# A two-layer graph network on one core: twelve dense chunks and three sums placed earlier in the first pass, and the nodes' own weighted terms added by VectorE instead of TensorE

## The reference

```python
h = max(layernorm(x), 0)
# layer 0: messages weighted by w_e, summed over the edges that end in a node
msg = h[dst] @ W_i + h[src] @ W_j + edge_attr @ W_e
x = x + segment_sum(w_e * msg, dst) + h @ W_self
h = max(layernorm(x), 0)
# layer 1, twice: mean over the neighbours, a product, a bias
h = relu(mean(h[src]) @ W1_l.T + b1 + h @ W1_r.T)
h = mean(h[src]) @ W2_l.T + b2 + h @ W2_r.T
x = x + log_softmax(h)
```

## Time and profile before

| | us |
|---|---|
| median of three runs | 1644.01 |
| profiled execution | 1642.16 |
| its span | 1640.3 |
| PE busy | 1422.1 |
| DVE busy | 971.8 |
| ACT busy | 605.0 |
| POOL busy | 716.3 |

### The profile page before, as it was taken

One profiled execution on the slowest core, in us unless ns is written; L12 is line 12 of the kernel. 1 busy time (PEld: TensorE's weight loads), 2 busy tenths in 40 slices (PEclk: granted clock), 3 DMA queues, 4 the chain that ended last, 5 costly groups with the idle time before them and its releaser, 6 DMA issues.

```text
span 1640.3 us, 26156 instructions
## 1 busy us (share of the span) xinstructions
PE 1422.1 (87%) x8546; PEld 1019.2 (62%) x8547; DVE 971.8 (59%) x4416; ACT 605.0 (37%) x1493; POOL 716.3 (44%) x769
## 2 busy tenths in 40 slices
PE   2588788788797988979879998999999979999996
PEld 0366666666575665756656668566666656666664
DVE  7798999997798987979798866200101130010204
ACT  5355565564645466455663346200000010020203
POOL 8777777776677776667676745000000000000000
PEclk9688899899998999989999999999999989999999
DMA  8477777888989888999889983687777748777773
GB/s 265 141 232 258 252 262 258 277 283 282 305 266 313 278 287 276 287 317 280 283 290 316 326 277 152 247 317 285 274 286 273 288 160 313 268 306 271 295 281 135
DMA packets 178854, 441.28 MB, mean 269 GB/s; under 512 B 24619, under 2 KB 104924, under 8 KB 175388
## 3 DMA queue, kind: packets, MB, share of 16 engines
q1 hardware_dynamic: 155996, 391.75, 66.4%
q0 software_dynamic: 22432, 46.97, 10.9%
q10 hardware_dynamic: 288, 0.85, 0.1%
HBM read 318.94 MB, written 120.55 MB: 268 GB/s over the span
## 4 chain that ended last, share of the span: by engine, by line
PE 64%; DVE 11%; DMA 10%; ACT 9%; issue 2%; POOL 2%; SPq 1%; DVEq 0%; ACTq 0%; POOLq 0%
PE psAE L1132 32%; PE psAE L1042 14%; DMA home<-h_table 8%; PE psAE L1074 6%; ACT home L789 4%; DVE home L1432 4%; PE psW L936 4%; DVE home L1436 3%; PE psW L1051 2%; DVE home L1490 2%; PE psW L1061 2%; ACT home L821 1%; PE psNS L1051 1%; PE psAE L1040 1%; ACT home L832 1%
## 5 line engine op out<-in xcount | busy, mean ns | idle before, releaser
L631 POOL DMA_INDIRECT home<-h_table,src_i x676 | 656.5, 971 | 266.4 <-issue 200.2
L1132 PE MATMUL psAE<-home 128*128 128x350 f16 x3528 | 538.2, 313 | 5.7 <-DVE home L1534 3.7
L1132 PEld LDWEIGHTS psAE<-home 128*128 128x128 f16 x3528 | 337.9, 96 | 200.9 <-issue 3.7
L1042 PE MATMUL psAE<-home 128*128 128x256 f32 x1352 | 322.9, 398 | 26.4 <-DVE home L1466 10.0
L1042 PEld LDWEIGHTS psAE<-home 128*128 128x128 f32 x1352 | 268.4, 201 | 78.8 <-issue 33.4
L1490 DVE TENSOR_SCALAR home<-iota_h,dst_rel,home 128x128 f32<-128x128 f16 x832 | 222.1, 363 | 17.2 <-PE psAE L1042 14.7
L1432 DVE TENSOR_SCALAR home<-iota_h,tile 128x245 f16<-128x245 f16 x1004 | 209.7, 303 | 27.7 <-PE psW L1061 18.8
L789 ACT ACTIVATE home<-psW 128x490 f16<-128x490 f32 x406 | 206.1, 577 | 51.7 <-PE psW L1051 38.7
L1436 DVE TENSOR_SCALAR home<-iota_h,tile 128x128 f16<-128x128 f16 x1004 | 179.3, 280 | 0.0
L1051 PE MATMUL psW<-home 128*128 128x245 f16 x812 | 126.0, 287 | 37.0 <-DVE home L1436 34.5
L1588 DVE SCALAR_TENSOR_TENSOR home<-psAE,home 128x350 f32<-128x350 f32 x18 | 9.4, 523 | 243.3 <-PE psAE L1132 238.5
(11 more groups left out here) (213 smaller groups left out, 1197.9 us busy)
## 6 DMA issues: line engine op xcount, KB each, us to landing
home<-counts SPq DMA_DIRECT2D x36, 4287.5 KB, 13.4
counts<-home SPq DMA_DIRECT2D x126, 612.5 KB, 4.8
home<-edges SPq DMA_DIRECT2D x64, 845.0 KB
weighted<-home SPq DMA_DIRECT2D x24, 1225.0 KB, 6.5
home<-weighted SPq DMA_DIRECT2D x36, 800.0 KB
home<-h_table,src_i POOLq DMA_INDIRECT x676
home<-h_table SPq DMA_DIRECT2D x36, 256.0 KB
home<-inv_row SPq DMA_DIRECT2D x36, 175.0 KB, 13.1
```

The costliest lines, as they stand in the source:

```text
L631: pool.indirect_dma_start(out=rows[to][:, j, :], out_offset=None, in_=from_table[:, :], in_offset=bass.IndirectOffsetOnAxis(ap=src_i[b][:, ...
L1042: done = nc.tensor.matmul(psA[:, 0:2 * P].rearrange("p (n f) -> p n f", n=2), onehot[:, j, :], both_of(s, b, j), start=(j == 0), stop=(j = ...
L1132: last = nc.tensor.matmul((psA, psE)[r][:, 0:SNODES].rearrange("p (c d) -> p c d", c=SUPER), halves[:, a, n, :], tiles[:, :, a, :], start= ...
```

## The change

Two things change. First, the tables of the first pass: the dense turns come earlier, and the three groups' pieces have other spans. Dense turns are now 3, 6, 9, 12, 16, 20, 25, 30, 35, 39, 44 and 49: the stretches from one to the next have 3 turns three times, 4 turns three times and 5 turns five times. Turns 50 to 63 are fourteen sourced ones. The first two groups' 26 pieces lie in turns 15 to 48, the last group's 13 in turns 50 to 62: two in turns 52 and 57, none in 51, one in each of the others. Second, the own weighted term leaves TensorE: GpSimd scales all 49 blocks, in order, and VectorE adds them to `x_sb`, one instruction of 7 blocks (896 columns) a step, and waits for its end before it adds the products. ScalarE's 14 scalings and TensorE's 49 identity matmuls are gone. (A single launch, the same inputs and outputs.)

```diff
-DENSE_AFTER = (2, 5, 9, 12, 16, 19, 23, 27, 30, 34, 38, 41)
-PIECE_SPANS = ((14, 29), (29, 43), (43, 51))
+DENSE_AFTER = (2, 4, 6, 8, 11, 14, 18, 22, 26, 29, 33, 37)
+PIECE_SPANS = ((11, 25), (25, 40), (40, 51))
...
                 pool.wait_ge(weight_kept, 1)
-                pool.wait_ge(own_back[1], 16)
-                for t in range(OWN_FIRST, BLOCKS):
-                    pool.tensor_scalar(accN[:, t * FEATS:(t + 1) * FEATS], accN[:, t * FEATS:(t + 1) * FEATS], node_weight[:, t:t + 1], None,
-                                       ALU.mult).then_inc(own_scaled, 1)
+                for n, (lo, hi) in enumerate(OWN_PARTS):
+                    pool.wait_ge(own_back[n], 16)
+                    for t in range(lo * UNROLL, hi * UNROLL):
+                        pool.tensor_scalar(accN[:, t * FEATS:(t + 1) * FEATS], accN[:, t * FEATS:(t + 1) * FEATS], node_weight[:, t:t + 1], None,
+                                           ALU.mult).then_inc(own_scaled, 1)
...
-                act.wait_ge(weight_kept, 1)
-                act.wait_ge(own_back[0], 16)
-                for t in range(OWN_FIRST):
-                    nc.scalar.activation(accN[:, t * FEATS:(t + 1) * FEATS], accN[:, t * FEATS:(t + 1) * FEATS], ACT.Copy,
-                                         scale=node_weight[:, t:t + 1]).then_inc(weight_kept, 1)
...
-                    if own:
-                        t = s * UNROLL + at + n
-                        if t < OWN_FIRST:
-                            pe.wait_ge(weight_kept, t + 2)
-                        else:
-                            pe.wait_ge(own_scaled, t - OWN_FIRST + 1)
-                        last = nc.tensor.matmul(bank[:, n * FEATS:(n + 1) * FEATS], ident[:, :], accN[:, columns], start=False, stop=True)
...
-            def first_rows():
+            def first_rows(scaled_own=False):
 
                 for s in range(STEPS + 2):
                     if s < STEPS:
+                        if scaled_own:
+                            own_columns = slice(s * UNROLL * FEATS, (s + 1) * UNROLL * FEATS)
+                            x_rows = x_sb[:, s * UNROLL:(s + 1) * UNROLL, :].rearrange("p t f -> p (t f)")
+                            dve.wait_ge(own_scaled, (s + 1) * UNROLL)
+                            nc.vector.tensor_tensor(x_rows, x_rows, accN[:, own_columns], ALU.add).then_inc(own_added, 1)
+                            dve.wait_ge(own_added, BLOCKS + s + 1)
```

More of the change, by code:

```diff
@@ L100 @@
 OWN_PARTS = ((0, 2), (2, 7))
-OWN_FIRST = OWN_PARTS[0][1] * UNROLL
 assert BLOCKS + OWN_ADDED < CHUNKS
@@ L929, in _, with products @@
                      1: ((hT, W1_R), (accA, W1_L)), 2: ((hT, W2_R), (accA, W2_L))}
-            def products(s, q, terms, bank, own=False):
+            def products(s, q, terms, bank):
                 at, width = PARTS[q]
@@ L936, in products @@
                         last = nc.tensor.matmul(bank[:, n * FEATS:(n + 1) * FEATS], frm[:, columns], w_sb[:, w, :],
-                                                start=(k == 0), stop=(k == len(terms) - 1 and not own))
-                    if own:
-                        t = s * UNROLL + at + n
-                        if t < OWN_FIRST:
-                            pe.wait_ge(weight_kept, t + 2)
-                        else:
-                            pe.wait_ge(own_scaled, t - OWN_FIRST + 1)
-                        last = nc.tensor.matmul(bank[:, n * FEATS:(n + 1) * FEATS], ident[:, :], accN[:, columns], start=False, stop=True)
+                                                start=(k == 0), stop=(k == len(terms) - 1))
                 return last
@@ L1106, in _, with mix_first @@
             fast = pe.value_load(fast_row[0:1, 0:1], min_val=0, max_val=1)
-            def mix_first(terms, own=False):
+            def mix_first(terms):
                 for s in range(STEPS + 2):
@@ L1115, in mix_first @@
                                 pe.wait_ge(mix_read[0], (s - 2) * UNROLL + at + width)
-                            products(s, q, terms, psB[s % 2 * 2 + q], own).then_inc(mixed[0], width)
+                            products(s, q, terms, psB[s % 2 * 2 + q]).then_inc(mixed[0], width)
                     if 2 <= s < LATE + 2:
@@ L1140, in _ @@
                 pe.wait_ge(added[0], ADDED)
-                mix_first(TERMS[0], True)
+                mix_first(TERMS[0])
                 for p in PASSES:
@@ L1623, in _ @@
                     nc.vector.memset(mark[:, p - 1:p], 0.0).then_inc(super_read[p], 2)
-                first_rows()
+                first_rows(True)
                 dve.wait_ge(deg_in, 16)
```

## The result

The changed kernel took 1662.46 us (median of four, 1659.42 to 1670.03), the kernel before, beside it, 1643.09 us (1641.2 to 1646.68): ratio 1.015, 95% interval 1.0116 to 1.0183, slower by 19 us between the medians and by 24.6 (19 to 30) by the ratio, which takes in further executions of the changed kernel, all between 1660 and 1675 us. A later comparison of the same two kernels gave 1.0109 (1.0081 to 1.0136), +18 us by the ratio and +16 between the medians. The forecast was +10.3 us: the sign was right, the size about half of what was measured.

A forecast was written before the change was run, and what follows sets the result against it. The first pass was taken as bound by compute, with late gathers bounding its end after the change; 12.8 us lost less 2.5 us gained gave +10.3 us, 1652.5 us on the profiled execution, 1654.3 us on the median, range 1637 to 1664.

The forecast's parts named there:

- What bounds the kernel: First pass: the compute side sets the pace, 12.1 us a sourced turn; GpSimd's 16.4 us sets have 5.6 us in reserve.
- The pieces: First pass: 26 pieces cost 36.7 us, mostly TensorE's load waits; cost kept for the new tables, bounds zero to 52.8 us.
- The last fourteen turns: First pass's end: gathers set the pace, turn 63 starting 193.2 us after turn 50, 12.8 us later than before.
- The compute side: Turns 50 to 63: compute work alone needs 180.7 us, hidden by the gathers' 193.2 us.
- Turn 50's start: First pass: turn 54's old start less four sourced turns of 12.1 us, 794.8 us; up to 3 us more allowed.
- The own term: Mixing stage: moving the own weighted term to GpSimd and VectorE gains about 2.5 us, bounds -4.5 to +1.
- TensorE's side of the round: Mixing stage: without identity matmuls the two-step chain of waits falls from 13.24 to 11.7 us, 5.8 a step.
- The shared port: Mixing stage: VectorE and GpSimd blocking each other would cost some 3 us; set aside because the trace does not show it.
- The sum: Whole kernel: 12.8 us lost in the first pass, 2.5 us gained in the mixing stage, +10.3 us.
- (1): Rival, turns 15 to 48: piece waits shrink with the earlier start, kernel faster; half the cost gone gives 1636; 14%.
- (2): Rival: GpSimd's lag is mostly made good by faster gathers, mixing and pieces, no change, 1644 to 1648 us; 20%.
- (3): Rival, ahead of turn 50: dense turns two sourced ones apart cost 5 us and more extra, 1660 to 1672 us; 10%.

The follow-up runs named there:

- the tables alone: Kernel before with only the new tables of dense turns and pieces, own weighted term unchanged: 1668.97 against 1645.39 us, 1.0136; on another chip 2013.01 against 2012.19 us.
- the end of them alone: Kernel before with tables changed only behind sourced chunk 23 (dense turns closer, last pieces over 11 turns): 1662.71 us, 1.011; on another chip 2012.64 us, 0.9989.
- the gathers thinned: Changed kernel, last twelve sets fetching 12 of 13 tiles: 1646.23 against 1637.08 us for the kernel before, 1.0054; on other chips 0.9913, 0.9917, 0.9924.
- the own term alone: Kernel before with only the own weighted term moved to GpSimd and VectorE, tables unchanged: 1644.14 us, 1.0; on another chip 2010.98 us, 0.9988.
- The spare matmuls: Kernel before with the own weighted term moved and six unused matmuls per mixing step: 1634.08 against 1635.75 us, 0.9992; on other chips 0.9985, 0.9988.
- early front: Kernel before with the first eight dense turns as in the changed kernel, last four and last pieces unchanged, own weighted term unchanged: 0.9991 and 1.0013.
- half the dose: Kernel before with the last dense turn after sourced chunk 39 instead of 41, twelve sourced turns at the end, own weighted term unchanged: 0.9977.

## Why the prediction was right or wrong

**What bounds the kernel** was read rightly: a set of gathers at 16.4 us against a sourced turn at 12.1 us, with dense turns as the balance and three sets as the limit of what can be saved up.

**The pieces were misread.** The 52.8 us of waits in the earlier trace rows add the idle time of the matmuls and that of the weight loads, which wait side by side. The matmuls alone, 330 to 843 us:

```profile
  DMA home<-h_table: 24.4, 12
```

and 3.6 us in 5 from there to turn 63. So the loads explain some two thirds of the 36.7 us that the first 26 pieces cost, and little of the 16.6 us of the last 13. Also, by the tables, the second group's last piece lies in turn 53 in the kernel before and in turn 50 in the changed one: 25 pieces lie ahead of turn 50 and 14 behind, where 26 and 13 were counted. Neither decides the forecast.

**The last fourteen turns: right.** Forecast 193.2 us from turn 50 to turn 63; measured 194.0, 192.5, 193.8 and 193.3 in four profiles on short chips (the changed kernel twice, the tables alone, the end of them alone). The kernel before took 131.95 us for the ten last turns; with four more at 12.1 us, 13.0 us of the loss lie here. Of the terms, the ten sets took 165.0 to 166.2 us (forecast 164.2 + 1.3 - 0.3 = 165.2). The second set began 24.6 to 24.7 us behind turn 50 in three profiles and 26.6 in one, instead of 26.1, and turn 63 came 2.1 to 3.3 us behind the last gather, instead of 1.9: two small errors that cancel, which was luck. In each of the four, every set from that one on began right behind the one before, ten sets long, where the kernel before has six. The compute side, put at 180.7 us, was too high: with the gathers thinned the stretch took 183.0 us, of which TensorE waited 12.2 us for gathers, and turns with one piece take as little as 11.8 us (53, 54 and 56 in the first profile of the changed kernel), where 13.4 was counted. It didn't matter, as the gathers hide it.

**Turn 50's start: the step that failed,** a mis-sized term. The prediction put it at 843.24 - 4 x 12.1 = 794.8 us. Five profiles on short chips have (the changed kernel twice, the tables alone, the end of them alone, the thinned one) 797.9, 801.7, 806.1, 802.0 and 799.5, mean 801.5: 6.7 us more. The subtraction keeps all that lay ahead of turn 54, its last dense turn too, which took 11.4 us. In the same five profiles that turn, now 49, took (start to start) 20.3, 17.7, 20.2, 16.1 and 18.5 us: 18.6 on average, 7.2 us more. This difference is clear of the spread: with the tables of before turn 53 took 11.4, 11.3 and 11.7 us in the three profiles on short chips. The stretches ahead of turn 49 cost on average what they should: 31, 38, 41 and 34 us over the sum without pieces in the four profiles with the changed tables, and 41 with the end of them alone, where 36.7 was carried over. But that average rests on values that lie far apart; with the tables of before the same figure is 37, 47 and 30 us, and turn 54 begins at 843.2, 853.8 and 836.8. So turn 49 accounts for the surplus of the mean, not for that of one profile.

I had seen that 11.4 was low, and allowed 3 us in the bounds, by an average over all turns. The rows of before would have given the number. Its dense turns with a piece (21, 25, 30, 35, 39, 44, 49, 53) take 15.7 us on average, and the three of them that follow a turn without a piece (21, 30, 44) take 19.1, 18.4 and 18.2, 18.6 on average. Turn 49 of the changed tables has a piece and follows a turn without one. What TensorE waits for in turn 49 of the second profile, in the middle of the turn:

```profile
792.04 0.40 PE L982 MATMUL psW<-home,ones 128*1 128x100 f32 x2 [3.47 <-ACT home L789]
...
797.26 2.95 PE L1062 MATMUL psAE<-home 128*128 128x400 f32 x8 [1.22 <-DMA home<-h_table]
```

ScalarE had itself waited 4.67 us for a store to `counts` there. In all eight profiles on short chips the 25 dense turns with a piece behind a turn without one take 17.7 to 20.5 us, and the 39 behind a turn that has one 11.2 to 17.6. So the tables' pattern of pieces goes with most of the loss here; no run changed it alone, so it isn't shown to be the cause. And it can't be all of it: in the end of the tables alone, turn 49 follows a turn with a piece, and took 16.1 us, 4.7 more than 11.4.

**The own term: the gain was put too high.** -2.5 us forecast. In the two profiles of the changed kernel the part behind turn 63 is 3.3 and 1.0 us shorter than in the kernel before, in the own term alone 0.3 us; over all profiles of each kind the gain is 0.9 us, and the time of the own term alone is 0.0% (4 us either way). The step that failed is the 5.8 us a step for TensorE's side of the round. The round of 11.7 us does occur, in the first profile of the changed kernel:

```profile
1017.29 5.21 PE L931 MATMUL psW<-w_sb,home 128*128 128x128 f32 x28
...
1030.09 0.95 PE L920 MATMUL psNS<-ident,home 128*128 128x128 f32 x7 [3.20 <-ACT home L860]
1030.88 3.29 PE L931 MATMUL psW<-w_sb,home 128*128 128x128 f32 x28
...
1041.76 0.95 PE L920 MATMUL psNS<-ident,home 128*128 128x128 f32 x7 [1.88 <-ACT home L860]
```

From 1030.09 to 1041.76 us it takes 11.67 us. But the sum took the matmuls off and kept the clock. With fewer of them the granted clock of this half fell to 0.91 here, 0.85 in the second profile and 0.87 in the own term alone, and in one step of each the 28 product matmuls took 4.4 to 5.2 us instead of 3.29 (above, at 1017.29). A step at that time or later then takes 7.2 to 7.8 us, longer than the 6.7 of before. Where the low clock reached the next stage, as in the own term alone, its 98 matmuls took 1.5 us more too. The spare matmuls brought the clock to 0.94 and above and left no step over 6.4 us behind the first: the stage's end (second group of line 1132, 1120 and 1122) came 68.2 to 69.8 us behind turn 63, where the kernel before has 72.4. The kernel's own spread limits this: two runs with the own term as before (early front once, half the dose), have 70.6 and 70.3. So the clock's part is shown in the rows, and not in the time.

**The shared port.** The Trainium skill (SBUF — State Buffer, "Who interferes with whom") calls the ports that the two engines share an exclusive lock. The prediction set this aside because VectorE's line 1534 took 1.06 us with GpSimd busy and without. That looked at one side only. GpSimd's rows in the kernel before show the other, one beside the instruction at 1002.80 and one beside that at 1009.47:

```profile
1003.10 1.23 POOL L684 TENSOR_SCALAR home<-home,node_weight 128x128 f32<-128x128 f32 x1
...
1009.52 1.48 POOL L684 TENSOR_SCALAR home<-home,node_weight 128x128 f32<-128x128 f32 x1
```

Its others take 0.59 to 0.60 us. So the two contend, as that section says, and for GpSimd a lock fits the rows, here and in the changed kernel (2.12 us where two VectorE instructions follow each other). For VectorE it fits only in part: its instruction at 1004.08 us, begun 0.05 us behind a GpSimd instruction of 0.59, took 0.17 us more than alone and not 0.54. The longer GpSimd's instruction had been under way, the less was added: 0.06 us at 0.19 us (VectorE's at 1031.07), nothing at 0.28 (at 1002.80 in the kernel before). The price of the edit was some 0.9 us of VectorE, spread over the stage, and not 3 us; GpSimd's 6.4 us (34.78 against 49 starts of 0.58) cost nothing, as VectorE waited for it only once, for the first seven blocks.

**The sum:** 13.0 + 6.7 - 1 = 18.7 us, against 19.4 and 16.1 us between the medians, and 24.6 and 17.9 by the ratios. What the first comparison's ratio has beyond it stays open. **Rivals:** the piece waits did not shrink (1); nothing was made good (2); the crowded front (3) cost little that was seen: in the first profile the stretches of three turns took 137 us against 3 x 44.1 = 132, 5 us that are part of the 31 above. The run that would have priced it alone fell on long chips.

## What to carry to other kernels

Two engines that feed each other through a few buffers have to be balanced over every stretch as long as the buffers last, not over the whole: cheap work spent early, while the feeder's buffers are full, is missing at the end. When a turn is taken out of a sequence, don't inherit the neighbours' measured times: look at how far they spread first. When two engines share something, read the rows of both, one instruction at a time: a mean over a group hides the few that were held up. And TensorE's work off the critical path may be holding its clock; take it away and look at the granted clock of that stretch and of the next.

## What was not expected of the hardware

**Chips of two sorts.** On four of seven chips the first pass was 355 to 370 us longer, with DMA packets and gathers as long as elsewhere (0.96 us a gather). In a profile of the changed kernel there (span 2010.4 us), ScalarE's copy starts 5 us behind the end of the multiplication it waits for. TensorE, then ScalarE:

```profile
1240.08 5.77 PE L1030 MATMUL psAE<-home 128*128 128x256 f32 x26
1245.70 0.58 PE L1039 MATMUL psW<-home 128*128 128x245 f16 x4
```

```profile
1250.89 0.39 ACT L768 ACTIVATE home<-psAE 128x256 f32<-128x256 f32 x1 [12.57 <-remote]
```

"remote" is a release for which the profile has no instruction that ended just before: the release came late, and VectorE, which waits for the same, began at 1250.84 us. GpSimd's rows say when it came:

```profile
1247.42 0.95 POOL L630 DMA_INDIRECT home<-h_table,src_i  x1 [0.30 <-issue]
1251.63 0.95 POOL L630 DMA_INDIRECT home<-h_table,src_i  x1 [3.26 <-remote]
```

The first is the last gather of a set. Its end, 1248.37 us, lies 2.5 us ahead of ScalarE's copy. The same distance is 2.5 to 2.9 us for each of the last nine sets, and GpSimd itself begins no set, from the eighth on, sooner than 2.7 us behind the end of the one before, where on short chips many follow by 0.3 us. So in this profile the waits of a sourced turn end some 2.6 us behind a set of gathers, and the turn is a set (16.1 us) and some 2.8 us. That the gathers hold up the releases is inferred from these times, and not shown by a run of its own; it fits the thinned runs, where twelve gathers of 1.26 us less, 15.1 us in all, gave 14.6 to 17.2 us in the last turns. It is still so that a turn there is longer than a set, that the buffers don't run out (TensorE waits for gathered rows once, at the start of the pass) and that no table makes a difference. But gathers are not without effect there, as had been expected: the turn is made of them. Why some chips do this, the runs don't say.
